# A two-layer graph network kernel: the second layer's PSUM banks and the steps of its dense sums

## The chip, the cores and the metric

The kernel runs on one core of one Trainium2 chip. The metric is the device time of one execution in microseconds (us); lower is better. Before the change three runs took 3727.17, 3734.83 and 3735.6 us, median 3734.83 us. A core has a matrix engine (PE; its weight loads are listed as PEld), a vector engine (DVE), a scalar engine (ACT), GpSimd (POOL) and SyncE (SP, which issues DMAs here). Each runs its own list of instructions strictly in order, and they meet through semaphores. PE writes its products to PSUM, which has eight banks of 128 x 512 fp32; DVE and ACT read them there.

## The reference, cut to what matters

```python
xn = layernorm(x)                                   # 6250 x 256
norm = w * rsqrt(deg_out[src] * deg_in[dst] + eps)  # 206250 edges
h6 = relu(segment_sum((xn @ W6)[src] * norm, dst) + b6)
h7 = relu(segment_sum((h6 @ W7)[src] * norm, dst) + b7)
x  = x + (h7 @ Wp + bp) + linear_attention(xn)
x  = x + mixture_of_experts(layernorm(x))           # 2 of 8 experts, 256 -> 512 -> 256
```

The change touches the second of the two `segment_sum` lines and what is computed beside it.

## The kernel before, in words

The edges are sorted by destination and cut into tiles of 128. A sum over edges is done in two ways at once.

*Run groups.* For 36 groups of 24 tiles in the second layer, POOL gathers the 128 source rows of each tile from DRAM by an indirect DMA (L1954, four per step, into a ring `msg` of six steps). PE multiplies the rows by small 128 x 32 matrices `Sb` (function `mm`, L659, four products a step) that DVE makes two steps ahead (`equal`, `weigh_S`, L1213 and L1228). After six steps a group is read by ACT, transposed by PE (`turn`, L647) and added by DVE to a sliding window `acc` (L1244).

*Dense chunks.* 26 chunks of edges are written as a whole matrix A (6250 sources by 128 destinations) and multiplied with the features X that lie in SBUF: 50 products per chunk, each 125x128 by 125x256 (function `dense`, L698; a product of fp32 operands is two instructions in the trace, so a chunk has 100). They add up in one PSUM bank, number 3. Then comes what I call the **boundary** of a chunk: ACT copies the bank to SBUF (`lift_chunk`, L1709), PE transposes it twice back into bank 3 (`dense_turn`, L706 and L708), DVE adds it to `acc` (`add_chunk`, L1253), and only then may the next chunk's first product write bank 3: `dense` waits for that addition.

21 of the 26 matrices were stored in DRAM in layer 1. SP loads each again (`load_A`, L2033, two DMAs of 1.6 MB) into one of two buffers, once the chunk before last is multiplied. Five ("extra groups" in the title) are built during layer 2: DVE makes one-hot matrices (`hots1`, L1274 and L1276), PE multiplies them (`build`, L676, 24 per chunk, four a step over six steps), and ACT evicts the results into A (`evict`, L1729 to L1735). Their builds take two banks in turn, 4 and 5.

*The stream.* As the windows of `acc` are complete, blocks of four row tiles (13 of them) go through the rest of the layer, one segment a step: `scl`, `hid0`, `relu0`, `hid1`, `relu1`, `out0`, `add0`, `out2`, `add2` with `stat`, `aggr`, `inv`, `norm`, `tr0`, `cp0`, `tr1`, `cp1`. PE's parts are L803 (hid, bank 2), L815 and L818 (out, bank 6) and L827 (tr, bank 7). The last block has banks 0, 1 and 3.

The order of work is fixed by hand in steps. Layer 2 has 234 steps, 0 to 233; steps 0 to 215 have an `mm`. Tables made at the top of the file tell which step does what: `AT1[c]` is the step at which chunk c starts (4, 12, 20, 28, ... up to 214), `MULT_AT[1]` holds the dense products of each step, `BUILD_AT[1]` the builds, `FIN_AT[1]` the boundary, `STREAM_AT` the stream. Every engine goes through the same steps. Before the change chunk c is multiplied in the steps `AT1[c] + 1` to `AT1[c + 1] - 1`, seven products in most steps; ACT lifts it at the end of that last step, and PE turns it and DVE adds it in step `AT1[c + 1]`, in which no dense product stands. Within a step PE does `mm`, one build, the turn of a chunk, two dense products, the turn of a run group, the other dense products and builds, and then the stream:

```python
if s < NQS[L]:
    mm(L, s)
for t in b[:1]:
    build(t)
if s in FIN_AT[L]:
    dense_turn(L, FIN_AT[L][s])
for d, k in m[:2]:
    dense(L, d, k)
```

Of the kernel before, what the change touches and what calls it, by code (L numbers as in the profile page):

```python
# [11 lines left out]
P = 128  # L12
W = 32
QT = 4
R = 125
# [100 lines left out]
FROM1 = 4  # L116
SPAN1 = NQS[1] - 2 - FROM1
assert NX == NY
# [25 lines left out]
for _c, _d in enumerate(CH[1]):  # L144
    if _d >= DY:
        for _t in range(size_of(_d)):
            BUILD_AT[1].setdefault(AT1[_c - 1] + 1 + _t * YB // size_of(_d), []).append(tile_of(_d) + _t)
    for _k in range(NT):
        MULT_AT[1].setdefault(AT1[_c] + 1 + _k * (AT1[_c + 1] - AT1[_c] - 1) // NT, []).append((_c, _k))
    FIN_AT[1][AT1[_c + 1]] = _c  # L150
PARTS = [("r", j) for j in range(NR)] + [("c", d) for d in range(DX)]
# [117 lines left out]
def gnn_block(nc, srcT, srcR, dstT, dstR, dstO, wO, wT, x, W6, b6, W7, b7, Wp, bp, wkvT, woT, wq, bo, lng, lnb,  # L269
              Wr, br, W1, b1, W2, b2, gamma, beta, need, out):  # L270
    ctx = ExitStack()
    with ctx:
# [251 lines left out]
        def bank_of(t):  # L524
            return (4, 5)[t % 2] if t >= tile_of(DY) else (2, 7, 5)[t % 3]

        def banks(t):
            return 2 if t >= tile_of(DY) else 3

# [41 lines left out]
        def pe_program(e):  # L571
# [107 lines left out]
            def dense(L, d, k):  # L679
                wd = XC if L == 0 else D  # L680
                if k == 0:
                    if L == 0:
                        e.wait_ge(s_ev, tile_of(d + 1))
                        e.wait_ge(s_r0, r0_before(tile_of(d + 1)))
                        e.wait_ge(s_xs, NT)
                    else:
                        e.wait_ge(l_xr, 16 * 5)
                    if L == 0 and d >= 1:
                        e.wait_ge(s_add, ADD_NO[0]["c", d - 1] + 1)
                    if L == 1 and d >= 1:  # L690
                        e.wait_ge(s_add, NU[0] + ADD_NO[1]["c", CH[1][d - 1]] + 1)
                    if L == 1 and CH[1][d] >= DY:
                        e.wait_ge(s_ev, tile_of(CH[1][d] + 1))
                        e.wait_ge(s_r0, r0_before(tile_of(CH[1][d] + 1)))
                if L == 1 and k % 25 == 0 and CH[1][d] < DY:
                    e.wait_ge(l_ap[(ND + d) % 2][k // 25], 16 * loaded(d))
                lhs = A[d % 2 if L == 0 else (ND + d) % 2][:, k, :]
                ins = e.matmul(PS[3][:, 0:wd], lhs, X[0:R, k, 0:wd], start=k == 0, stop=k == NT - 1)  # L698
                if k % 10 == 9:
                    ins.then_inc(s_mul, 1)  # L700

            def dense_turn(L, d):
                bank = PS[3]
                e.wait_ge(s_lc, L * ND + d + 1)
                if L == 0:
                    e.matmul(bank[:, 2 * P:3 * P], agd[:, D:D + 1].to_broadcast([P, P]), ident[:, :], start=True, stop=True)  # L706
                for h in range(2):
                    ins = e.transpose(bank[:, h * P:(h + 1) * P], agd[:, h * P:(h + 1) * P], ident[:, :])  # L708
                ins.then_inc(s_tc, 1)

            def sums(L, s):
# [4 lines left out]
                for t in b[:1]:  # L716
                    build(t)
                if s in FIN_AT[L]:
                    dense_turn(L, FIN_AT[L][s])
                for d, k in m[:2]:  # L720
# [69 lines left out]
            def stream(c, seg, slowly):  # L790
                (i0, n), k = CHUNKS[c], c % 2
                j, ci = half(c)
                wd, c0 = n * R, base_col(i0 * R)
                B_hid, B_out, B_tr = (PS[b] for b in ((0, 1, 3) if j else (2, 6, 7)))
                if seg in ("hid0", "hid1"):
                    m = int(seg[-1])
                    if not slowly:
                        e.wait_ge(c_scl, c + 1)
                    if 2 * ci + m >= 1:
                        e.wait_ge(c_relu[j], 2 * ci + m)  # L800
                    for h in range(2):
                        rhs = accs[:, h, i0 * R:i0 * R + wd] if slowly else acc[:, h, c0:c0 + wd]
                        ins = e.matmul(B_hid[:, 0:wd], w7[:, h, m * P:(m + 1) * P], rhs, start=h == 0, stop=h == 1)  # L803
                    ins.then_inc(c_hid[j], 1)
# [91 lines left out]
        def dve_program(e):  # L896
# [351 lines left out]
            def add_chunk(L, d):  # L1248
# [3 lines left out]
                o, n = (acc if L else acc3)[:, :, bass.ds(b, P)], 2 if L else 3  # L1252
                e.tensor_tensor(o, o, PS[3][:, 0:n * P].rearrange("p (h c) -> p h c", h=n), ALU.add).then_inc(s_add, 1)  # L1253
                added[0] += 1
# [358 lines left out]
        def act_program(e):  # L1613
# [90 lines left out]
            def lift_chunk(L, d):  # L1704
                wd = XC if L == 0 else D
                e.wait_ge(s_mul, 5 * (L * ND + d + 1))
                if L * ND + d >= 1:
                    e.wait_ge(s_tc, L * ND + d)
                e.activation(agd[:, 0:wd], PS[3][:, 0:wd], ACT.Copy).then_inc(s_lc, 1)  # L1709

# [90 lines left out]
            with e.Else():  # L1801
# [3 lines left out]
                for s in range(STEPS0):  # L1805
# [9 lines left out]
                    if s in HID_AT:  # L1815
                        degree_root(HID_AT[s])
                    if s + 1 in FIN_AT[0]:
                        lift_chunk(0, FIN_AT[0][s + 1])
                    for group in tables_at(0, s):
# [9 lines left out]
            def stream(c, seg):  # L1829
                (i0, n), k = CHUNKS[c], c % 2  # L1830
                j, ci = half(c)
                wd = n * R
                B_hid, B_tr = (PS[0], PS[3]) if j else (PS[2], PS[7])
                if seg in ("relu0", "relu1"):
# [22 lines left out]
            with e.Else():  # L1857
                for s in range(STEPS1):
# [4 lines left out]
                    for c, seg in STREAM_AT.get(s, ()):  # L1863
                        stream(c, seg)
                    if s + 1 in FIN_AT[1]:
                        lift_chunk(1, FIN_AT[1][s + 1])
                    clear1(s)
# [382 lines left out]
```

## Time and profile before

| | |
|---|---|
| median of three runs | 3734.83 us (3727.17 to 3735.6) |
| the profiled execution's own time | 3725.99 us |
| its span, first to last instruction | 3724.2 us |
| granted clock of PE over the span | 0.907 of full speed |
| PE busy with products | 2986.8 us (80%) |
| POOL busy | 2168.3 us (58%) |
| DVE busy, ACT busy | 1807.5 us (49%), 1147.4 us (31%) |

Times inside the trace are counted from the start of the span. The products of layer 2 begin at 2034.9 us, its last dense product ends at 3318.8 us, and from about 3350 us on the experts run. The clock is one of two levels, 1.0 (2.4 GHz) or 0.5 (1.2 GHz); a mean between them tells how long each was granted. The start of a product is recorded, its end is modelled, and the signal that tells the other engines of it can come later than that end.

### The profile page before, as it was taken

Reading aid. Unit: us, or ns where it says so; the run is one execution under the profiler, and the core shown is the slowest. Engines: PE = TensorE matmul, PEld = TensorE weight load, DVE = VectorE, ACT = ScalarE, POOL = GpSimd, SP = SyncE. Lnnn points to the kernel's source line nnn. Section 1 sums busy time; section 2 is a strip of 40 time slices with the busy share of each in tenths; the row PEclk is TensorE's granted clock in tenths of the full one; section 3 lists DMA queues with packets and bytes.
Section 4 is the critical chain, followed back from the end, with each engine's and each line's share of the span. In section 5 each row is a group of like instructions: output and inputs, shape, how many; then the busy total and the mean of one; then the engine's idle time right before and its main releaser. Section 6 shows DMA issues by size and latency. Waiting matters only on the chain.

```text
span 3724.2 us, 52328 instructions
## 1 busy us (share of the span) xinstructions
PE 2986.8 (80%) x16152; PEld 1996.9 (54%) x16152; DVE 1807.5 (49%) x4528; ACT 1147.4 (31%) x4063; POOL 2168.3 (58%) x2090
## 2 busy tenths in 40 slices
PE   4777837888888888878874688888888888888998
PEld 3445514555555555555542356555555555555666
DVE  9989835666666666656542133223222424222334
ACT  5777834443444444444330011001000101002211
POOL 4666656666666777666664666665666666630000
PEclk8899967998999999999996789889988989998999
DMA  4331134544545445445455535553555454533221
GB/s 118 98 102 57 56 78 132 173 140 137 173 138 163 150 139 173 135 142 167 129 194 177 124 126 168 192 187 106 193 193 191 148 192 149 190 101 106 78 77 47
DMA packets 219543, 515.58 MB, mean 138 GB/s; under 512 B 62465, under 2 KB 129831, under 8 KB 208169
## 3 DMA queue, kind: packets, MB, share of 16 engines
q0 software_dynamic: 88704, 243.35, 22.8%
q1 hardware_dynamic: 124053, 262.34, 20.7%
q10 hardware_dynamic: 6500, 6.40, 0.6%
q8 instruction: 141, 2.31, 0.2%
q14 instruction: 145, 1.19, 0.1%
HBM read 384.88 MB, written 127.07 MB: 137 GB/s over the span
## 4 chain that ended last, share of the span: by engine, by line
PE 33%; another core or an unknown queue 11%; issue 4%; DVE 3%; DMA 1%; ACT 1%; DVEq 0%; POOL 0%; SPq 0%; ACTq 0%; POOLq 0%
PE ps L698 13%; PE ps L867 5%; PE ps L880 4%; PE ps L659 3%; PE ps L676 3%; PE ps L818 1%; PE ps L815 1%; PE ps L803 1%; PE ps L708 0%; PE ps L638 0%; DVE wb L1274 0%; PE ps L827 0%; DVE accb L1244 0%; DVE ab L1297 0%
## 5 line engine op out<-in xcount | busy, mean ns | idle before, releaser
L1954 POOL DMA_INDIRECT ringb<-t,src x1848 | 1859.2, 1006 | 984.6 <-issue 494.6
L698 PE MATMUL ps<-xb,ab 125*128 125x256 f32 (+1 forms) x4700 | 1229.6, 402 | 87.3 <-issue 85.4
L698 PEld LDWEIGHTS ps<-xb,ab 125*128 125x128 f32 x4700 | 927.6, 201 | 355.1 <-issue 194.0
L676 PE MATMUL ps<-mlb 128*125 128x300 f32 x1260 | 476.9, 470 | 160.7 <-ACT side L1735 63.0
L1731 ACT ACTIVATE ab<-ps 125x250 f32 x724 | 294.7, 407 | 827.8 <-PE ps L676 410.7
L659 PE MATMUL ps<-ringb,Sb 128*32 128x257 f32 (+1 forms) x3696 | 358.7, 419 | 112.5 <-issue 46.3
L676 PEld LDWEIGHTS ps<-mlb 128*125 128x125 f32 x1260 | 224.6, 201 | 324.1 <-issue 281.6
L1927 POOL TENSOR_TENSOR ab<-ab,wn 128x100 f32<-128x100 f32 x201 | 274.1, 1369 | 169.5 <-DVE ab L1080 169.5
L600 PE MATMUL ps<-ab 128*50 128x125 f32 x3228 | 221.4, 284 | 135.6 <-ACT ab L1653 47.3
L1264 DVE TENSOR_TENSOR mlb<-iof,rel 128x900 f32<-128x900 f32 (+1 forms) x231 | 232.3, 1006 | 186.7 <-remote 129.9
L1653 ACT ACTIVATE ab<-ab,wn 128x50 f32<-128x50 f32 x1212 | 286.8, 328 | 21.1 <-DVE ab L1080 21.0
L600 PEld LDWEIGHTS ps<-ab 128*50 128x50 f32 x3228 | 180.6, 131 | 199.9 <-issue 100.5
L1213 DVE TENSOR_TENSOR Sb<-iof,rel 128x128 f32<-128x128 f32 x462 | 131.2, 284 | 292.4 <-remote 147.8
L1297 DVE TENSOR_TENSOR ab<-ab,side 125x50 f32 x724 | 177.6, 245 | 167.8 <-DVE ab L1297 77.0
L659 PEld LDWEIGHTS ps<-ringb,Sb 128*32 128x32 f32 x3696 | 86.2, 111 | 312.4 <-issue 235.8
L1082 DVE TENSOR_TENSOR ab<-iof,ringb 128x1000 f32<-128x1000 f32 x202 | 247.8, 1227 | 0.0
L1244 DVE TENSOR_TENSOR accb<-accb,ps 128x96 f32 (+1 forms) x308 | 73.8, 240 | 351.1 <-remote 248.3
L1959 POOL TENSOR_TENSOR rs<-mv,consts 125x4 f32<-125x4 f32 (+1 forms) x13 | 12.9, 989 | 394.4 <-DVE mv L1600 394.4
L1745 ACT ACTIVATE mlb<-mlb,wn 128x125 f32<-128x125 f32 x630 | 207.0, 393 | 92.7 <-issue 55.2
L867 PE MATMUL ps<-xb 128*128 128x500 f32 (+1 forms) x416 | 172.1, 572 | 4.1 <-DMA Sb<-in_b 3.6
L880 PE MATMUL ps<-xb,ab 128*125 128x256 f32 x800 | 174.6, 379 | 0.0
L880 PEld LDWEIGHTS ps<-xb,ab 128*125 128x125 f32 x800 | 150.2, 188 | 26.9 <-issue 5.1
(245 smaller groups left out, 2704.3 us busy)
## 6 DMA issues: line engine op xcount, KB each, us to landing
ad<-ab SPq DMA_DIRECT2D x42, 1600.0 KB
ab<-ad SPq DMA_DIRECT2D x42, 1600.0 KB
ringb<-t,src POOLq DMA_INDIRECT x1848
kvd<-mlb SPq DMA_DIRECT2D x50, 256.0 KB, 2.1
kvb<-kvd SPq DMA_DIRECT2D x50, 256.0 KB
x2t<-mlb SPq DMA_DIRECT2D x13, 500.0 KB
xb<-x2t SPq DMA_DIRECT2D x13, 500.0 KB, 8.2
xb<-in_x SPq DMA_DIRECT2D x10, 625.0 KB
```

What stands on the lines that cost most here:

```text
L600: ins = e.matmul(PS[j % 2][o:o + NT, 0:R], hot_w[:, r, j, :], hot_lo[:, r, j, :], start=t0 + j < 2, stop=t0 + j >= T - 2)
L659: ins = e.matmul(PS[g % 2][k * W:(k + 1) * W, 0:wd], Sb[:, qi % NS, k, :], msg[:, slot * QT + k, 0:wd], start=r == 0, stop=r == GR - 1)
L676: e.matmul(PS[bank_of(t)][0:R, 0:HR], low[:, slot_of(t), :], high[:, slot_of(t), :], start=True, stop=True).then_inc(s_bld, 1)
L698: ins = e.matmul(PS[3][:, 0:wd], lhs, X[0:R, k, 0:wd], start=k == 0, stop=k == NT - 1)
L867: ins = e.matmul(PS[j][:, 0:wd], M1[:, k, h, j * P:(j + 1) * P], XF[c % RF][:, h, 0:wd], start=h == 0, stop=h == 1)
L880: ins = e.matmul(pb[0:R, t * D:(t + 1) * D], hT[:, rr, m, (t0 + t) * R:(t0 + t + 1) * R], M2[:, m // 4, m % 4, :], start=m == 0, stop=m == 7)
L1082: e.tensor_tensor(hot_lo[:, r, 0:n, :], iof[:, 0:R].unsqueeze(1).to_broadcast([P, n, R]), lo_f[:, t0:t0 + n].unsqueeze(2).to_broadcast([P, ...
L1264: e.tensor_tensor(Mb[:, o:o + n, :], iof[:, 0:HR].unsqueeze(1).to_broadcast([P, n, HR]), rel[:, c0:c0 + n].unsqueeze(2).to_broadcast([P, n ...
L1653: e.activation(hot_w[:, r, j, :], hot_hi[:, r, j, :], ACT.Copy, scale=wn[:, t0 + j:t0 + j + 1]).then_inc(s_wa, 1)
L1731: e.activation(A1[place][:, :, bass.ds(b, RT - 1)], bank[:, :, 1:RT], ACT.Copy).then_inc(s_ev, 1)
L1927: e.tensor_tensor(hot_w[:, c % RD, NA:n, :], hot_hi[:, c % RD, NA:n, :], wn[:, t0 + NA:t0 + n].unsqueeze(2).to_broadcast([P, n - NA, NT]), ...
L1954: e.indirect_dma_start(msg[:, slot * QT + k, 0:width], None, table, bass.IndirectOffsetOnAxis(src[:, t:t + 1], 0)).then_inc(s_g[slot], 16)
```

## The change

It applies to the second layer alone (L = 1); for layer 1 every table and bank stays.

- *Dense chunks* alternate between banks 3 and 7. Chunk c waits for the addition of chunk c - 2 instead of c - 1. The products now fill the steps `AT1[c]` to `AT1[c + 1] - 1`, so none is left out, with six or seven a step. `FIN_AT` moves two steps on: ACT lifts chunk c in step `AT1[c + 1]`, PE turns it in `AT1[c + 1] + 1` (`FIN_AHEAD`), DVE adds it in `AT1[c + 1] + 2`. `AT1` is spread over one step less (the last chunk ends in step 212 instead of 213).
- *The stream* of all blocks but the last uses bank 6 for hid, out and tr. `hid0` of a block waits in addition until ACT has copied `cp1` of the block before.
- *Builds* of the five extra groups take banks 2, 4 and 5 in turn; a build waits for the eviction of the third before it instead of the second.

```diff
-SPAN1 = NQS[1] - 2 - FROM1
+SPAN1 = NQS[1] - 3 - FROM1
...
-        MULT_AT[1].setdefault(AT1[_c] + 1 + _k * (AT1[_c + 1] - AT1[_c] - 1) // NT, []).append((_c, _k))
-    FIN_AT[1][AT1[_c + 1]] = _c
+        MULT_AT[1].setdefault(AT1[_c] + _k * (AT1[_c + 1] - AT1[_c]) // NT, []).append((_c, _k))
+    FIN_AT[1][AT1[_c + 1] + 2] = _c
+FIN_AHEAD = [0, 1]
...
         def bank_of(t):
-            return (4, 5)[t % 2] if t >= tile_of(DY) else (2, 7, 5)[t % 3]
+            return (2, 4, 5)[t % 3] if t >= tile_of(DY) else (2, 7, 5)[t % 3]
+
+        def dense_bank(L, d):
+            return (3, 7)[d % 2] if L else 3
 
         def banks(t):
-            return 2 if t >= tile_of(DY) else 3
+            return 3
...
-                    if L == 1 and d >= 1:
-                        e.wait_ge(s_add, NU[0] + ADD_NO[1]["c", CH[1][d - 1]] + 1)
+                    if L == 1 and d >= 2:
+                        e.wait_ge(s_add, NU[0] + ADD_NO[1]["c", CH[1][d - 2]] + 1)
...
-                ins = e.matmul(PS[3][:, 0:wd], lhs, X[0:R, k, 0:wd], start=k == 0, stop=k == NT - 1)
+                ins = e.matmul(PS[dense_bank(L, d)][:, 0:wd], lhs, X[0:R, k, 0:wd], start=k == 0, stop=k == NT - 1)
...
-                if s in FIN_AT[L]:
-                    dense_turn(L, FIN_AT[L][s])
+                if s + FIN_AHEAD[L] in FIN_AT[L]:
+                    dense_turn(L, FIN_AT[L][s + FIN_AHEAD[L]])
...
-                B_hid, B_out, B_tr = (PS[b] for b in ((0, 1, 3) if j else (2, 6, 7)))
+                B_hid, B_out, B_tr = (PS[b] for b in ((0, 1, 3) if j else (6, 6, 6)))
...
                         e.wait_ge(c_relu[j], 2 * ci + m)
+                    if m == 0 and ci >= 1:
+                        e.wait_ge(c_cp[j], 2 * ci)
...
-                    if s + 1 in FIN_AT[1]:
-                        lift_chunk(1, FIN_AT[1][s + 1])
+                    if s + 1 + FIN_AHEAD[1] in FIN_AT[1]:
+                        lift_chunk(1, FIN_AT[1][s + 1 + FIN_AHEAD[1]])
```

`dense_turn`, `add_chunk`, `lift_chunk` and ACT's half of the stream take the same new banks.

## Rows read from the trace of the kernel before

**Rows 1.** The profile's page: span and busy times.
```profile
span 3724.2 us, 52328 instructions
PE 2986.8 (80%) x16152; PEld 1996.9 (54%) x16152; DVE 1807.5 (49%) x4528; ACT 1147.4 (31%) x4063; POOL 2168.3 (58%) x2090
...
q8 instruction: 141, 2.31, 0.2%
```

**Rows 2.** Busy time by stretch: length, each engine (instructions), clock, DMA share, GB/s.
```profile
2034.90:2126.00 91.10, 51.34 (x221) 28.97 (x222) 10.13 (x35) 3.95 (x4) 60.84 (x64) 0.67 0.57 139
2126.00:3319.00 1193.00, 1001.49 (x4984) 688.22 (x4983) 343.56 (x1118) 119.44 (x372) 765.31 (x793) 0.91 0.51 165
```

**Rows 3.** PE's waits, 2100 to 3330: total us, times, longest.
```profile
PE ps L698 <- issue: 68.8, 68, 5.0
PE ps L708 <- ACT agd L1709: 46.9, 11, 9.7
PE ps L659 <- issue: 24.8, 37, 2.2
PE ps L676 <- DVE wb L1276: 14.4, 8, 5.5
PE ps L676 <- DVE wb L1274: 10.4, 7, 5.0
PE ps L676 <- ACT side L1735: 8.4, 5, 5.2
PE ps L708 <- issue: 6.6, 4, 3.0
```

**Rows 4.** POOL's gathers by source line, 2100 to 3330: durations, then idle before.
```profile
L1954 POOL DMA_INDIRECT ringb<-t,src x809: 943/949/1922, 2099.7 to 3309.3; - x162
...
  issue: 218.0, 711
  remote: 123.4, 53
  PE ps L659: 87.9, 45
```

**Rows 5.** Busy time in the ten boundaries shorter than 5 us.
```profile
2405.35:2409.27 3.92, 1.51 (x19) 0.48 (x19) 0.52 (x3) 0.66 (x2) 3.00 (x4) 1.00 0.89 287
...
sum 34.76, PE 22.71 PEld 7.83 DVE 7.94 ACT 7.46 POOL 23.55; mean PE 2.27 PEld 0.78 DVE 0.79 ACT 0.75 POOL 2.36
```

**Rows 6.** Busy time in the fifteen boundaries of 5 us and more.
```profile
2212.76:2225.01 12.25, 3.40 (x22) 1.41 (x22) 3.64 (x13) 3.14 (x2) 7.64 (x8) 0.60 0.30 86
...
2497.88:2506.42 8.54, 1.61 (x20) 0.48 (x19) 1.26 (x8) 0.68 (x2) 6.41 (x8) 0.74 0.75 263
...
sum 136.33, PE 58.18 PEld 25.52 DVE 25.23 ACT 24.48 POOL 86.90; mean PE 3.88 PEld 1.70 DVE 1.68 ACT 1.63 POOL 5.79
```

**Rows 7.** Timeline of one boundary: start, length, engine, line, idle before.
```profile
2495.56 2.33 PE L698 MATMUL ps<-xb,ab 125*128 125x256 f32 x10
...
2500.68 0.80 SPq L2033 DMA_DIRECT2D ab<-ad  x2
2500.68 0.38 ACT L1709 ACTIVATE agd<-ps 128x256 f32<-128x256 f32 x1 [2.31 <-remote]
...
2501.12 0.44 PE L708 MATMUL ps<-ident,agd 128*128 128x128 f32 x2 [2.66 <-ACT agd L1709]
...
2505.89 0.42 DVE L1253 TENSOR_TENSOR accb<-accb,ps 128x256 f32 x1 [7.17 <-remote]
...
2506.42 6.55 PE L698 MATMUL ps<-xb,ab 125*128 125x256 f32 x16 [4.26 <-issue]
...
2513.47 3.30 PE L698 MATMUL ps<-xb,ab 125*128 125x256 f32 x14
```

**Rows 8.** Timeline: a block's cp1 on ACT, the next block's hid0 on PE.
```profile
2530.86 0.20 ACT L1848 ACTIVATION_READ_ACCUMULATOR mlb<-ps 128x1 f32 x1
...
2543.64 1.90 PE L803 MATMUL ps<-accb,kvb 128*128 128x500 f32 x4
```

More of the change, by code:

```diff
@@ L702, in dense_turn @@
             def dense_turn(L, d):
-                bank = PS[3]
+                bank = PS[dense_bank(L, d)]
                 e.wait_ge(s_lc, L * ND + d + 1)
@@ L1252, in add_chunk @@
                 o, n = (acc if L else acc3)[:, :, bass.ds(b, P)], 2 if L else 3
-                e.tensor_tensor(o, o, PS[3][:, 0:n * P].rearrange("p (h c) -> p h c", h=n), ALU.add).then_inc(s_add, 1)
+                e.tensor_tensor(o, o, PS[dense_bank(L, d)][:, 0:n * P].rearrange("p (h c) -> p h c", h=n), ALU.add).then_inc(s_add, 1)
                 added[0] += 1
@@ L1708, in lift_chunk @@
                     e.wait_ge(s_tc, L * ND + d)
-                e.activation(agd[:, 0:wd], PS[3][:, 0:wd], ACT.Copy).then_inc(s_lc, 1)
+                e.activation(agd[:, 0:wd], PS[dense_bank(L, d)][:, 0:wd], ACT.Copy).then_inc(s_lc, 1)
             tile_columns = TileColumns(e, "at")
@@ L1816, in act_program @@
                         degree_root(HID_AT[s])
-                    if s + 1 in FIN_AT[0]:
-                        lift_chunk(0, FIN_AT[0][s + 1])
+                    if s + 1 + FIN_AHEAD[0] in FIN_AT[0]:
+                        lift_chunk(0, FIN_AT[0][s + 1 + FIN_AHEAD[0]])
                     for group in tables_at(0, s):
@@ L1832, in stream @@
                 wd = n * R
-                B_hid, B_tr = (PS[0], PS[3]) if j else (PS[2], PS[7])
+                B_hid, B_tr = (PS[0], PS[3]) if j else (PS[6], PS[6])
                 if seg in ("relu0", "relu1"):
```

## The prediction

> **What bounds the kernel now.** I read the page first, then busy time by stretch, then the waits of PE and of POOL in layer 2, then the boundaries between dense chunks one by one. The page shows PE as the busiest engine, 2986.8 us of a span of 3724.2 us, POOL next with 2168.3 us [rows 1]. The change touches only layer 2. Its dense part runs from 2034.9 to about 3319 us, 1284.1 us in two stretches: 91.1 us of start, in which PE is busy for 51.34 us at a mean clock of 0.67, and 1193 us in which it is busy for 1001.49 us at 0.91 [rows 2].
>
> Who holds whom in those 1193 us? A step has four gathers of 949 ns, and at least 0.30 us lies before each (218.0 us over 711 waits), so POOL needs 4 x 1.25 = 5.0 us a step; 216 steps are 1080 us, against the 1284 us that they take. The rest is POOL waiting: 123.4 us for a releaser that the trace can't name and 87.9 us for PE's products L659, 211 us in all, which are waits for a free place in the ring [rows 4]. Among PE's waits of the same stretch none is for a gather; they are for its own issue, for ACT's lift L1709, and for the builds' inputs [rows 3]. So PE sets the pace, and POOL is up to a ring behind it with some 200 us to spare. What PE saves in this stretch comes off the end, until POOL's 1080 us are reached.
>
> PE loses time at the boundaries. From the end of a chunk's last dense product to the start of the next chunk's first there are 25 of them: ten short ones of 34.76 us with 22.71 us of PE work (run-group products, turns, stream) [rows 5], fifteen long ones of 136.33 us with 58.18 us [rows 6]. Idle: 12.05 and 78.15 us, 90.2 us together. The timeline of one shows the chain: the last products end at 2497.89, ACT lifts at 2500.68, when the signal has come (SP starts the next load of A at the very same time, so it is the signal that is late and not ACT), PE turns at 2501.12, DVE adds at 2505.89 to 2506.31, and the next dense product starts at 2506.42, at the lower clock: 16 instructions in 6.55 us, where 14 take 3.30 us at full clock later, which is 3.77 us for 16 [rows 7].
>
> **The change part by part.**
>
> *Dense banks in turn, boundary two steps later.* Removed are the wait for the addition of the chunk just done and, as far as one step of PE work covers it, the wait of the turn for the lift. No instruction is added to PE: 50 products, two transposes, one lift and one addition a chunk, as before. What goes has three terms.
> 1. What every boundary costs, even where the signal is prompt: 12.05 / 10 = 1.2 us idle [rows 5]. 25 x 1.2 = 30 us. The lift (0.38 us), the turn and the addition (0.42 us) now lie beside dense products of the other bank. I take all of it.
> 2. What the late signals add at the long ones: 78.15 - 15 x 1.2 = 60 us [rows 6]. Here I have to choose. If the lateness belongs to the round trip from PE to ACT to PE to DVE to PE, all 60 us go. If PE itself is held up (it waits 68.8 us in dense products and 24.8 us in run products on nothing but issue [rows 3]), the delay comes back inside a chunk, where the gain is 0. I can't tell them apart, and take half, 30 us.
> 3. The clock. Behind the boundary of [rows 7] the 16 instructions cost 6.55 - 3.77 = 2.8 us more. Twelve of the fifteen long boundaries have a mean clock under 0.90 (between 0.60 and 0.89; two of them stand in [rows 6]), so up to 12 x 2.8 = 34 us. It goes with the idle time of term 2; half, 17 us.
> Sum: 77 us. From both sides: term 1 alone, 30 us, if the delays return; 30 + 60 + 34 = 124 us if everything goes.
>
> *Next behind the turn.* The turn stands after `mm` and one build of the step after the lift, and a step of six or seven dense products and an `mm` is some 4 us of PE work at full clock (14 instructions in 3.30 us and the `mm`). The longest wait of the turn for the lift is 9.7 us [rows 3], so a rest of up to some 5 us stays at the worst boundaries; that is inside the half of term 2.
>
> *Loads of A.* The load of chunk c still starts when chunk c - 2 is multiplied, but chunk c starts one step earlier, eight steps later instead of nine. Two DMAs of 1.6 MB at the 287 GB/s of the boundary stretch at 2405 us [rows 5] are about 11 us against eight steps of at least 5.0 us. Cost 0; if the cover were gone, PE would wait for the second half of A. SP's queue issues it at the same place, and no other DMA moves by more than a step.
>
> *Stream in one bank.* Inside a block the bank was already handed on by waits (relu before the next hid, add before the next out, norm before tr), so the one new wait is `hid0` for the `cp1` before. In the trace cp1 of a block ends at 2531.06 and the next block's first hid product starts at 2543.64 [rows 8]: 12.6 us of slack over two steps. Behind this wait on PE stand the run products, for which POOL waits. I price it at 0; were all the slack gone, each of the 11 such waits would cost at most the part of a step that ACT is late. The banks 2 and 7 that it frees are what makes the other two edits possible.
>
> *Builds in three banks.* PE waits 14.4 + 10.4 us before builds for DVE's one-hot matrices, which three banks don't change, and 8.4 us for ACT's eviction (L1735), which they may take away [rows 3]. Against it stands that PE no longer gives DVE a pause before the builds of the five extra chunks: five boundaries' 1.2 us, 6 us, may come back as waits for DVE. I take -2 us for the two together, between a gain of 8 and a loss of 6.
>
> *Start and end.* Dense products begin in step 4 instead of 5, in a stretch where PE is busy for 56% [rows 2]: a gain of a few us at most, 0 in the sum, since the 91 us there are set by gathers and a low clock. The last chunk ends a step earlier and is added a step later (215 for 214), before the stream's step 216 that needs it: 0. The number of steps stays 234.
>
> Sum: 77 - 2 = 75 us. 3725.99 - 75 = 3651 us for an execution like the profiled one; the median of the runs before, 3734.83, lies 8.8 us above that execution, so the forecast is 3734.8 - 75 = **3660 us**.
>
> *A rule against it.* POOL's spare time says that PE's idle time at boundaries is on the path [rows 4]. The Trainium skill, "TensorE: Matmul & The Clock Gate", section "HAM oscillation — how this bites in real kernels", reports of a tuned matmul kernel that double-buffering its PSUM gave no further gain (125.5 after 126.6 us); by that the sum would be about 0. That is rival 3. On term 2, the skill's "Runtime: NRT & Kernel Launch", section "Instruction fetch mechanics", holds that the cost of crossing a 16 KiB block of instructions is mostly hidden; 2.31 MB in 141 packets on the instruction queue q8 [rows 1] are such blocks. By that PE's waits on issue would not be its own supply, and all of term 2 would go (rival 1).
>
> **The rivals.**
> 1. *All of it goes*: 124 us and the 8 us of evictions, 3735 - 130 = 3605 us. For it: ACT and SP see the signal late together, and a pause in PE's work stands before each low clock. Against: issue waits also stand in the middle of chunks [rows 3].
> 2. *Only the fixed part goes*, 30 us, less the 6 us at extra chunks: 3711 us. For it: 93.6 us of issue waits that no bank explains [rows 3].
> 3. *No gain*: what PE saves it waits for elsewhere, for gathers or DVE, 3735 us. For it: the ring couples PE and POOL, and the load of A now meets a running PE with DMA shares of 0.75 to 0.92 [rows 5, 6]. Against: 1080 us of gathers against 1284 us.
> 4. *Slower*: the lift now follows ACT's stream segment of the step `AT1[c + 1]`. In 11 of the 26 boundaries that is a relu or a copy (steps 36, 52, 68, 84, 100, 116, 132, 180, 188, 204, 213), which itself waits for PE. If each held the turn, and with it the run products behind it, by as much as the longest wait of today, 9.7 us [rows 3], that is 107 us against the 75 gained: 3767 us. It decides once such a wait is over 6.8 us each. Against: each of these segments waits for a PE segment one step earlier.
>
> **How the numbers follow.** Forecast (gain of 45 to 110 us) 0.60; rival 1 0.10; rival 2 0.14; rival 3 0.09; rival 4 0.07. About 0.3%, 11 us, is what a measurement of this kernel can tell from no change. Rival 2 is mostly faster by that bound: faster 0.60 + 0.10 + 0.12 = 0.82, within 0.3% 0.02 + 0.08 = 0.10, slower 0.01 + 0.07 = 0.08. The range goes from 3608, nearly all of rival 1, to 3720, rival 2 with a margin of 9 us; outside remain rivals 3 and 4 and a tail of rival 1, some 0.2. The forecast's own range is 3625 to 3690.
>
> **What would show it.** In the trace after: PE's wait before L708, 53.5 us now (46.9 + 6.6), under 15 us, and no idle time of PE tied to L1253; the boundary stretches close to pure PE work; the stretch from the first run product to the last dense product down from 1284 to about 1210 us with a mean clock above 0.91; POOL's 211 us of waits down by about as much; builds' waits near 33 us; the time from the last dense product to the end unchanged. It is wrong if L708 waits as long as now (rival 4), if issue waits of L698 and L659 grow by what L708 loses (rival 2), or if PE begins to wait for gathers (rival 3).

## The result, and the profile after

The kernel after takes 3711.0 us (five runs, 3708.81 to 3720.0), the kernel before 3734.83 (five runs, 3727.17 to 3737.23): ratio 0.9946, 95% interval 0.9935 to 0.9958. It is 24 us faster, clear of the noise; the forecast was 75. The profiled execution of after is the slowest of its five (3720.0 us), that of before (3725.99) lies under all of its five, so the two traces lie only 6 us apart, and differences of a few us are not read from them.

The page of after, first lines [rows 1]:

```profile
span 3718.2 us, 52328 instructions
PE 3030.2 (81%) x16152; PEld 2012.8 (54%) x16152; DVE 1803.2 (48%) x4528; ACT 1150.8 (31%) x4063; POOL 2172.4 (58%) x2090
```

The same instructions, yet PE is "busy" for 43 us more. Layer 2's two stretches, columns as in [rows 2]:

```profile
2036.80:2128.00 91.20, 52.46 (x233) 30.55 (x234) 9.01 (x32) 3.53 (x3) 61.02 (x64) 0.67 0.59 140
2128.00:3311.00 1183.00, 1028.47 (x4953) 690.00 (x4952) 339.33 (x1116) 119.00 (x370) 767.85 (x792) 0.90 0.52 166
```

The second is 10 us shorter. PE's idle time in it fell from 191.5 to 154.5 us, its busy time rose from 1001.5 to 1028.5, and the clock did not rise (0.91, 0.90). PE's waits, 2100 to 3330 us: total, times, longest [rows 3]:

```profile
PE ps L702 <- issue: 59.0, 75, 1.8
PE ps L663 <- issue: 58.9, 75, 2.4
PE ps L680 <- DVE wb L1280: 9.6, 4, 5.5
...
PE ps L680 <- DVE wb L1282: 4.1, 3, 1.6
...
PE ps L712 <- ACT agd L1715: 1.9, 2, 1.5
PE ps L712 <- issue: 1.3, 3, 0.6
```

L702 is before's L698 (dense), L663 its L659 (run products), L680 its L676 (builds), L712 its L708 (turn). The wait of the turn is gone, 53.5 us to 3.2. What came in its place stands in the second line: run products wait 58.9 us on their issue ("issue": PE waits for nothing that the trace shows), 24.8 before. And POOL waits as much as ever for its ring, 137.5 + 64.3 = 201.8 us against 211.3 [rows 4] ("remote": a signal whose sender the trace can't name):

```profile
POOL ringb L1960 <- issue: 219.4, 715, 1.0
POOL ringb L1960 <- remote: 137.5, 60, 3.7
POOL ringb L1960 <- PE ps L663: 64.3, 36, 4.9
```

The timeline of after around the lift of one chunk (start, length, engine, line, idle before) answers to [rows 7]:

```profile
2507.30 0.38 PE L663 MATMUL ps<-ringb,Sb 128*32 128x256 f32 x1 [1.06 <-issue]
...
2509.40 0.38 PE L663 MATMUL ps<-ringb,Sb 128*32 128x256 f32 x1 [1.73 <-issue]
...
2510.11 1.11 PE L663 MATMUL ps<-ringb,Sb 128*32 128x256 f32 x4 [0.33 <-issue]
2510.21 0.79 SPq L2039 DMA_DIRECT2D ab<-ad  x2
2510.22 0.39 ACT L1715 ACTIVATE agd<-ps 128x256 f32<-128x256 f32 x1 [2.94 <-remote]
2510.31 0.29 DVE L1219 TENSOR_TENSOR Sb<-iof,rel 128x128 f32<-128x128 f32 x1 [0.98 <-remote]
2510.55 0.95 POOL L1960 DMA_INDIRECT ringb<-t,src  x1 [2.61 <-remote]
...
2511.14 0.69 PE L712 MATMUL ps<-ident,agd 128*128 128x128 f32 x2
```

The eight run products of one step, which have nothing to wait for between them, take from 2505.55 to 2511.22, in pieces. The last dense product of the chunk that is lifted ends at 2501.20, yet the trace has its signal at 2510.19, and ACT's lift, which waits for it, starts at 2510.22, 9.0 us late. SP, ACT, DVE and POOL all move within 0.34 us of each other. So two things are late: PE's own starts, and its signals to everyone, the latter also for products behind which PE went on for 4 us without a hole. Such holes also stand between dense products of one chunk: successive starts are 0.216 us apart at full clock and 0.427 at half, but 49 times over 0.6 us in before and 70 times in after, which by the starts in the traces costs 45 and 68 us beyond the usual distance.

The same lateness is what POOL waits for. In before the median distance from one gather's start to the next is 1.25 us; the 1284.5 us from the first of the 864 gathers to the last contain 87 pauses of over 2.2 us at the first gather of a step, the one that waits for PE's run products, and these hold 182 us more than 1.25 us each. Counted by the recorded ends of the products, the place in the ring had been free for 5.7 us (median) when such a pause ended; 81 of the 87 end 0.2 to 0.4 us after a recorded signal of PE's run products. In after it is 84 pauses with 175 us.

### The profile page after: what moved, and what is told of

It is laid out like the page before. It is cut to its first block, busy times and chain, and to the rows that moved or that the text cites. A ratio compares the mean times of both kernels' runs of the same rounds, so it can differ in the third digit from the quotient of the medians.

```text
span 3718.2 us, 52328 instructions
## 1 busy us (share of the span) xinstructions
PE 3030.2 (81%) x16152; PEld 2012.8 (54%) x16152; DVE 1803.2 (48%) x4528; ACT 1150.8 (31%) x4063; POOL 2172.4 (58%) x2090
## 4 chain that ended last, share of the span: by engine, by line
PE 46%; issue 8%; another core or an unknown queue 6%; DVE 3%; DMA 2%; ACT 1%; POOL 1%; DVEq 1%; ACTq 0%; SPq 0%; POOLq 0%
PE ps L702 19%; PE ps L680 7%; PE ps L663 5%; PE ps L873 5%; PE ps L886 4%; PE ps L821 1%; PE ps L824 1%; POOL ringb L1960 1%; PE ps L642 1%; PE ps L809 1%; ACT ab L1737 1%; DMA t<-mbuf 0%; DVE ab L1303 0%; DMA x2d<-accb 0%
## 5 line engine op out<-in xcount | busy, mean ns | idle before, releaser
L702 PE MATMUL ps<-xb,ab 125*128 125x256 f32 (+1 forms) x4700 | 1253.7, 407 | 83.3 <-issue 80.6
L702 PEld LDWEIGHTS ps<-xb,ab 125*128 125x128 f32 x4700 | 934.9, 203 | 358.5 <-issue 197.7
L680 PE MATMUL ps<-mlb 128*125 128x300 f32 x1260 | 484.1, 475 | 170.4 <-issue 67.9
L663 PE MATMUL ps<-ringb,Sb 128*32 128x257 f32 (+1 forms) x3696 | 378.2, 417 | 141.9 <-issue 78.2
L680 PEld LDWEIGHTS ps<-mlb 128*125 128x125 f32 x1260 | 228.1, 205 | 335.7 <-issue 298.1
L663 PEld LDWEIGHTS ps<-ringb,Sb 128*32 128x32 f32 x3696 | 90.5, 111 | 362.3 <-issue 290.3
```

The costliest lines, as they stand in the source:

```text
L663: ins = e.matmul(PS[g % 2][k * W:(k + 1) * W, 0:wd], Sb[:, qi % NS, k, :], msg[:, slot * QT + k, 0:wd], start=r == 0, stop=r == GR - 1)
L680: e.matmul(PS[bank_of(t)][0:R, 0:HR], low[:, slot_of(t), :], high[:, slot_of(t), :], start=True, stop=True).then_inc(s_bld, 1)
L702: ins = e.matmul(PS[dense_bank(L, d)][:, 0:wd], lhs, X[0:R, k, 0:wd], start=k == 0, stop=k == NT - 1)
```

## The experiments

Two kinds of chips took part, and the kernel before ran on each beside the experiments. On two "prompt" chips it took 3372.5 and 3370.9 us, on three "late" chips 3726.1, 3736.3 and 3734.5, as in the result. The names say only how soon PE's signals arrive in the traces. Ratios are to the kernel before on the same chip.

| run | chip | us | ratio, 95% interval |
|---|---|---|---|
| dense_alone | prompt 1 | 3371.5 | 0.9996 (0.9987 to 1.0004) |
| rest_alone | prompt 1 | 3373.2 | 1.0000 (0.9991 to 1.0008) |
| b_1g / a_1g | prompt 1 | 3225.9 / 3220.6 | 0.9565 (0.9551 to 0.9579) / 0.9543 (0.9527 to 0.9559) |
| change | prompt 2 | 3363.0 | 0.9976 (0.9965 to 0.9986) |
| b_lag | prompt 2 | 3368.4 | 0.9993 (0.9983 to 1.0003) |
| b_1g_lag / a_1g_lag | prompt 2 | 3297.6 / 3216.3 | 0.9780 (0.9765 to 0.9794) / 0.9539 (0.9525 to 0.9554) |
| b_ahead3 | late 1 | 3724.6 | 0.9992 (0.9980 to 1.0004) |
| a_ahead3 | late 1 | 3705.5 | 0.9950 (0.9926 to 0.9975) |
| b_1g_lag18 / a_1g_lag18 | late 1 | 3619.7 / 3520.1 | 0.9720 (0.9701 to 0.9739) / 0.9449 (0.9428 to 0.9470) |
| b_nold | late 2 | 3736.3 | 0.9997 (0.9986 to 1.0008) |
| a_nold | late 2 | 3720.0 | 0.9958 (0.9942 to 0.9975) |
| b_2g / a_2g | late 2 | 3400.7 / 3388.2 | 0.9098 (0.9078 to 0.9118) / 0.9061 (0.9046 to 0.9076) |
| b_5dense | late 3 | 3708.1 | 0.9917 (0.9886 to 0.9948) |
| b_3g | late 3 | 3487.1 | 0.9338 (0.9320 to 0.9356) |

**The halves of the change.** dense_alone is the kernel after with builds in two banks and the stream in 2, 6, 6; rest_alone is the kernel before with only the new banks of stream and builds.

```diff
 # dense_alone, from after
-            return (2, 4, 5)[t % 3] if t >= tile_of(DY) else (2, 7, 5)[t % 3]
+            return (4, 5)[t % 2] if t >= tile_of(DY) else (2, 7, 5)[t % 3]
...
-            return 3
+            return 2 if t >= tile_of(DY) else 3
...
-                B_hid, B_out, B_tr = (PS[b] for b in ((0, 1, 3) if j else (6, 6, 6)))
+                B_hid, B_out, B_tr = (PS[b] for b in ((0, 1, 3) if j else (2, 6, 6)))
...
```

> The dense chunks' part alone: banks 3 and 7 in turn, products in all steps, boundary two steps later. The stream keeps bank 2 for hid and has bank 6 for out and tr; builds keep two banks. Theory A (most of what the boundaries lost comes back as PE's own issue waits, and the bank sharing costs nothing): the whole gain of the change, 20 to 26 us, so 3709 to 3715 us. Rival B (the dense part brings 75 us and sharing bank 6 or the builds take 50 back): 3655 to 3675 us.

> The other two parts alone: the stream's products share bank 6 with the added wait, builds take banks 2, 4, 5; the dense chunks as before. Theory A: no change beyond 5 us, 3730 to 3740 us. Rival B: slower by some 50 us, 3785 us.

Neither moves the time on this chip. The expectations were written for a kernel before of 3735 us, so this does not decide between A and B; the halves ran on no late chip, and which of them brings the 24 us there is not shown. Waits of rest_alone in layer 2 (1900 to 2990 us), PE's and then POOL's:

```profile
PE ps L659 <- DMA ringb<-t,src: 100.7, 48, 7.0
PE ps L676 <- DVE wb L1276: 5.1, 6, 1.1
PE ps L698 <- issue: 1.7, 7, 0.5
```

```profile
POOL ringb L1956 <- issue: 249.7, 819, 0.3
POOL ringb L1956 <- PE ps L659: 4.6, 15, 0.3
```

Here PE waits for gathers, POOL for nothing but its own issue, and there are no holes. The gathers set the pace: their median distance is 1.25 us, as in before, but only 2 pauses are longer than 2.2 us. What PE saves at a boundary, it waits for at the next gather.

**PE in front.** b_1g and a_1g issue one gather of four in layer 2, so that PE is the last on any chip.

```diff
-                    for k in range(QT):
+                    for k in range(1 if L else QT):
...
```

PE's wait for the gathers is set to the smaller number in the same way.

> The kernel before with one of the four gathers of each step in layer 2, as in a_1g. The difference to a_1g is what the change is worth when PE alone sets the pace. Theory C: 50 to 100 us slower than a_1g (each of the 25 boundaries costs its 1.2 us idle, a part of the late signals and of the clock). If the difference is 20 to 30 us as on the full kernels, the boundaries never cost more than that, and the gathers took nothing back.

> The changed kernel with one of the four gathers of each step in layer 2; the other three are left out, so three quarters of the run groups' rows are stale. Theory C (PE's issue waits come while POOL issues gathers without a pause, and end when POOL has to wait): with a quarter of the gathers POOL waits in every step, the issue waits of PE in layer 2 (118 us) shrink to under 30 us, the clock stays high, and layer 2 runs near PE's work, some 945 us at full clock from the first run product to the last dense one: 3400 to 3470 us. Rival D (the issue waits are PE's own supply of instructions): the same number of instructions, so the issue waits stay at some 100 us, and the time is over 3600 us.

The difference of the two kernels is 5.3 us, where b_1g's expectation had 50 to 100. The 3400 to 3470 us of a_1g's theory C were meant for a late chip, and this chip has no holes to take away, so that run does not decide between C and D. Busy time by stretch of b_1g: one boundary, and the sum over its 25:

```profile
1959.68:1961.38 1.70, 1.51 (x19) 0.47 (x19) 0.42 (x1) 0.66 (x2) 0.83 (x1) 1.00 0.63 120
sum 71.77, PE 65.75 PEld 28.44 DVE 27.76 ACT 31.03 POOL 25.34; mean PE 2.63 PEld 1.14 DVE 1.11 ACT 1.24 POOL 1.01
```

71.77 - 65.75 = 6.0 us of idle time, 0.24 us a boundary, at full clock: that is all that a boundary costs where signals are prompt, and the change returns it.

**An artificial late signal.** Six more lifts ahead of the one that counts:

```diff
+                for r in range(6 if L else 0):
+                    e.activation(agd[:, 0:wd], PS[3][:, 0:wd], ACT.Copy).then_inc(s_lag, 1)
+                    e.wait_ge(s_lag, 6 * d + r + 1)
                 e.activation(agd[:, 0:wd], PS[3][:, 0:wd], ACT.Copy).then_inc(s_lc, 1)
```

> The kernel before with one gather of four a step in layer 2 (three quarters of its products read stale rows), and six more lifts of each of layer 2's chunks ahead of the one that counts, each waiting for the one before: an artificial late signal of about 6 x 0.5 = 3 us in each of the 25 boundaries, in a kernel in which PE sets the pace. Theory B (the boundary of the kernel before puts the whole of PE's idle time at each boundary on the path, and it is 0.24 us in each where signals are prompt): 25 x 3 = 75 us more than the 3225.9 us without the lag, 3290 to 3310 us. Rival R (a lag is made up by work queued elsewhere, so a late signal costs little even in the kernel before): under 3245 us.

> The same six more lifts for each chunk, and one gather of four, in the kernel after. Theory B: the turn stands a step, 4.3 us of PE work, behind the lift, so a lag of 3 us is covered nearly everywhere: within 8 us of the 3220.6 us without it. Rival S (the lag is not covered, because ACT starts the lift late in its step behind its stream segment or behind evictions): 30 us or more.

> The kernel before with all four gathers and the same six more lifts a chunk. Theory G at a kernel before of about 3370 us: in the dense part of 1061 us PE is busy for 962, so POOL's pace hides part of the 75 us: 5 to 45 us more. Where the kernel before takes about 3730 us and PE sets the pace: 60 us or more. Rival P (PE sets the pace on this chip too): 75 us more whatever the chip.

b_1g_lag pays 71.7 us, 2.9 a boundary; a_1g_lag nothing (-4.3; the two runs without the lag were on the other prompt chip). Theory B holds: where PE sets the pace, a late lift is paid in full before and hidden after. PE's wait for the lift in b_1g_lag, then in a_1g_lag:

```profile
PE ps L709 <- ACT agd L1713: 53.2, 26, 2.5
```

```profile
PE ps L713 <- ACT agd L1719: 2.0, 1, 2.0
```

b_lag has the same 25 late lifts, and PE waits 47.8 us for them in the dense part, but with all four gathers the time doesn't move at all. I had expected 5 to 45 us. The wait for gathers shrinks instead, from 100.7 us in rest_alone to 51.4:

```profile
PE ps L660 <- DMA ringb<-t,src: 51.4, 29, 4.5
PE ps L709 <- ACT agd L1713: 47.8, 25, 2.5
```

How far does the cover reach? Eighteen more lifts:

> The kernel before with one gather of four a step in layer 2 and eighteen more lifts of each chunk ahead of the one that counts. Six of them cost 71.7 us (3297.6 against 3225.9), 2.9 us in each of 25 boundaries; eighteen make a signal that is 8.6 us late, near the longest wait for a lift in the kernel before (9.7 us). Theory B: 3226 + 25 x 8.6 = 3441 us, 3425 to 3455. Rival R: under 3400 us.

> The same eighteen more lifts in the kernel after, one gather of four. Theory B with the price that the prediction put on a long signal (the turn stands a step of 4.3 us and a run product behind the lift, some 5 us in all): 8.6 - 5 = 3.6 us stay at each of 25, so 3216 + 90 = 3306 us, 3285 to 3330. Rival T (the cover is longer, up to two steps, because the work between is at least two steps): under 3235 us. Rival S (no cover left once the signal is later than the step): over 3400 us.

These ran on a late chip, where layer 1 with all its gathers takes 160 us more, so the totals miss what I wrote and the dense part is compared (b_1g_lag18, then a_1g_lag18):

```profile
2048.40:3208.00 1159.60, 978.37 (x5148) 691.91 (x5148) 345.26 (x1140) 294.96 (x824) 199.25 (x204) 0.91 0.32 105
```

```profile
2051.10:3110.00 1058.90, 966.00 (x5145) 689.31 (x5146) 343.77 (x1138) 294.71 (x823) 201.69 (x205) 0.95 0.35 115
```

Without lag the two take 930 and 924 us. So a signal that costs 230 / 25 = 9.2 us before costs 135 / 25 = 5.4 after: the change covers 3.8 us of lateness at each boundary. The prediction had some 5 us of cover. Theory B had 215 and 90 us for the two; it is right in kind, but the 135 us of after lie over its range of 69 to 114. R, S and T fall. With one gather of four neither trace has a hole between dense products, though the chip is a late one.

**The whole change on a prompt chip.**

> The change as a whole, run again beside the kernel before, since the times of the experiments' first chip (3372.5 us for the kernel before) differ by a tenth from those in which the change brought 24 us (3734.8 us). Theory G (POOL's gathers set the pace of layer 2 where no signal is late: 1061 us of dense part against 216 steps at about 5.2 us of gathers): a ratio of 0.998 to 1.001 if the kernel before takes about 3370 us again. If the kernel before takes about 3730 us: 0.993 to 0.996. Rival W (the whole is worth more than its two halves, which measured 0.9996 and 1.0000): a gain of 10 us or more at 3370 us.

8 us faster, 5 to 12 by its interval. Theory G had a ratio of 0.998 or more, Rival W a gain of 10 us or more; it lies between, and the interval reaches both. From first to last dense product it takes 1057 us, against 1062 and 1063 for the halves on the other prompt chip. The trace nearest to the kernel before on this chip is that of b_lag, at 0.9993 of its time: in both, layer 2's run products begin at 1865 us, and the last dense product ends at 2949.6 in change and at 2958.3 in b_lag, so the gain lies inside the dense part. Why the whole brings what neither half does is not shown.

**A shorter lead of POOL.**

```diff
-                        e.wait_ge(s_mm, L * NQ + j - RQ + 1)
+                        e.wait_ge(s_mm, L * NQ + j - (3 if L else RQ) + 1)
...
```

> The kernel before with POOL's gathers of layer 2 kept at most three steps ahead of PE's run products instead of six (the ring's depth). It asks what the ring's spare places hide. Theory G (POOL sets the pace and PE follows it closely, so the ring is seldom more than three steps full): within 10 us of the kernel before. Rival H (what a late PE costs is made up out of the ring's six places; with three, each of the 25 boundaries reaches POOL): 15 to 50 us slower. Where the kernel before takes about 3730 us, theory C (PE is held up while POOL runs on through a dozen gathers, and a shorter lead breaks this up): 20 us faster or more; its rival there: slower.

> The kernel after with the same lead of three steps. Theory G: within 10 us of the kernel before, and within 8 us of b_ahead3. Rival H: faster than b_ahead3 by 15 us or more, since the boundary that reaches POOL there is gone here.

Nothing moves: b_ahead3 as before, a_ahead3 0.9950 as the change itself, 19 us under b_ahead3. Theory C falls. Rival H falls for b_ahead3, which should have been 15 to 50 us slower; that a_ahead3 is 15 us or more faster, as it had it, is only the gain that the change has without the shorter lead. Theory G holds for b_ahead3 and misses a_ahead3 (within 8 us). The holes are fewer (30 of over 0.6 us instead of 49, and 20 in a_ahead3), and PE waits 72.9 us for gathers instead, 104.4 in a_ahead3. POOL pauses as before, 90 times for 184 us. That was the first sign that on a late chip, too, something other than PE's work keeps the time.

**The loads of A, and half of the gathers.** b_nold and a_nold leave out layer 2's refills of A; b_2g and a_2g issue two gathers of four.

```diff
...
-                if s in refill:
-                    load_A(refill[s])
```

> The kernel before without layer 2's refills of A (19 chunks are multiplied with what the two buffers held): all four gathers. If the kernel before takes about 3726 us: theory Y: the holes go, and the dense part falls to POOL's pace of about 1100 us, 3560 to 3620 us in all; theory X: it stays within 40 us of the kernel before. If the kernel before takes about 3372 us: POOL's pace is unchanged, 3350 to 3375 us.

> The kernel after without layer 2's refills of A. Theory X at 3726 us: 15 to 30 us under b_nold, as the full kernels are. Theory Y at 3726 us: within 10 us of b_nold, as both then follow POOL. At a kernel before of 3372 us: within 8 us of b_nold.

> The kernel before with two gathers of four a step in layer 2 (half of its products read stale rows). POOL then needs 216 x 2.5 = 540 us and PE sets the pace. If the kernel before takes about 3726 us: theory X (holes come with the gathers' rate): the dense part falls from 1257 to 930 to 1000 us, 3400 to 3470 us in all, with few holes; theory Y (the loads of A bring them): the dense part stays over 1100 us, 3570 or more. If the kernel before takes about 3372 us there are no holes to explain, and PE's pace gives 3226 us, as with one gather, 3220 to 3240.

> The kernel after with two gathers of four. Under theory X, or at a kernel before of 3372 us, its advantage over b_2g is that of prompt boundaries, 0.24 x 25 = 6 us, 2 to 12 us. Under theory Y at 3726 us it is that of the full kernels, 15 to 30 us.

Theory Y falls, and the loads have no part in it: b_nold has the time of before, its holes (39) and its waits, and a_nold is 16 us under it. Half of the gathers gone, every hole is gone. Dense part of b_2g, then POOL's waits and PE's:

```profile
2059.00:2990.00 931.00, 920.55 (x5148) 660.45 (x5148) 345.03 (x1140) 123.21 (x374) 400.34 (x408) 1.00 0.49 159
```

```profile
POOL ringb L1954 <- PE ps L659: 408.5, 167, 7.2
...
POOL ringb L1954 <- issue: 84.2, 223, 4.4
```

```profile
PE ps L698 <- issue: 3.0, 14, 0.5
```

This is how a stretch looks in which PE does set the pace: 99% busy, clock 1.00, nearly all of POOL's waiting named after PE's product, no "remote". POOL issues its next gather a median of 0.3 us after the product that frees the place; in the kernel before it is 5.3 us after it. Theory X, that the holes come with the rate of the gathers, holds; it says nothing of how. The change is worth 12.5 us in total here, just over the 2 to 12 expected, and 6.8 us in the dense part (931.0 to 924.2). The two profiled executions lie only 2.7 us apart, so they can't tell where the other 6 are.

**Which way the link runs.** b_5dense keeps every gather and load and takes 45 of 50 dense products of each chunk away.

```diff
+                if L == 1 and k % 10 != 9:
+                    return
...
```

b_3g issues three gathers of four.

> The kernel before with 5 of 50 dense products in each chunk of layer 2 (the dense sums lack the other 45), all four gathers, all loads. PE's work in the dense part falls by about 1170 x 2 x 0.216 = 505 us, so PE can't set the pace. If the kernel before takes about 3735 us: theory Z (the gathers have a pace of 1.49 us each of their own): the time stays within 25 us of the kernel before, 3705 to 3745. Theory V (PE's dense work and the gathers disturb each other): the gathers go at the 1103 us of the other chips, 3540 to 3570 us. If the kernel before takes about 3372 us: within 10 us of it, as POOL's gathers set the pace.

> The kernel before with three gathers of four. If the kernel before takes about 3735 us: theory Z: 648 x 1.49 = 964 us from the first gather to the last, near PE's own 930 us of dense part, so 3400 to 3440 us and few holes. Theory V with a disturbance that grows with the gathers: the dense part half way between 930 and 1257 us, 3500 to 3600 us. If the kernel before takes about 3372 us: 648 x 1.28 = 827 us, below PE's 930, so PE's 3226 us, 3220 to 3240.

With nearly all dense work gone the time falls by 26 us, to 3708 us. PE's dense part, PE's waits and POOL's:

```profile
2075.60:3304.00 1228.40, 637.30 (x2804) 289.22 (x2800) 348.28 (x1141) 123.28 (x375) 805.08 (x832) 0.66 0.53 166
```

```profile
PE ps L659 <- issue: 118.6, 97, 5.8
PE ps L659 <- DMA ringb<-t,src: 68.4, 20, 18.1
PE ps L710 <- ACT agd L1711: 63.5, 8, 16.5
```

```profile
POOL ringb L1956 <- issue: 230.3, 755, 0.5
POOL ringb L1956 <- remote: 132.6, 42, 5.8
POOL ringb L1956 <- PE ps L659: 46.6, 20, 8.5
```

PE is idle for half of it, and still every engine waits for late signals, PE's turn for ACT's lift for 16.5 us at worst. One such place in the timeline of b_5dense:

```profile
2209.06 0.59 PE L659 MATMUL ps<-ringb,Sb 128*32 128x256 f32 x1 [0.83 <-issue]
...
2216.55 0.94 POOL L1956 DMA_INDIRECT ringb<-t,src  x1 [0.30 <-issue]
2221.94 0.38 ACT L1711 ACTIVATE agd<-ps 128x256 f32<-128x256 f32 x1 [28.08 <-remote]
2221.96 0.94 POOL L1956 DMA_INDIRECT ringb<-t,src  x1 [4.46 <-remote]
2222.10 1.28 DVE L1246 TENSOR_TENSOR accb<-accb,ps 128x64 f32 x4 [13.12 <-remote]
2222.38 0.69 PE L710 MATMUL ps<-ident,agd 128*128 128x128 f32 x2 [12.74 <-issue]
```

The last dense product of the chunk that ACT lifts ends at 2202.02, the run products that free the place for which POOL waits (those of step 26) at 2197.94, and PE's last product before the gap at 2209.64. ACT, POOL, DVE and PE go on together at 2221.94 to 2222.38; the trace has the signal of that dense product at 2221.92, 19.9 us late.

The gathers take as long as before. Their line by source, with first and last start at its end, in before, b_5dense and rest_alone (prompt):

```profile
L1954 POOL DMA_INDIRECT ringb<-t,src x864: 943/949/1922, 2024.8 to 3309.3; - x173
```

```profile
L1956 POOL DMA_INDIRECT ringb<-t,src x864: 940/946/1957, 2035.0 to 3299.3; - x173
```

```profile
L1956 POOL DMA_INDIRECT ringb<-t,src x864: 942/949/1992, 1862.4 to 2963.1; - x173
```

1284.5, 1264.3 and 1100.7 us. On late chips it is between 1264 and 1289 us in all seven kernels with four gathers (after 1279.2, b_ahead3 1284.9, a_ahead3 1276.8, b_nold 1288.6, a_nold 1279.7), whatever PE has to do. Theory Z has the time right (3708 in 3705 to 3745), theory V falls. But what Z says of the reason, a pace of 1.49 us that the gathers have of their own, the traces refute: in each of these kernels the median distance between gathers is 1.25 us, as on the prompt chips, and the rest is pauses at the ring, 182 us in before and 166 us in b_5dense (55 pauses, and there the place had been free for 15.5 us). The same holds for b_3g, which by Z should have had 964 us of gathers and 3400 to 3440 us, and by V 3500 to 3600; it has

```profile
L1954 POOL DMA_INDIRECT ringb<-t,src x648: 943/949/1969, 2028.5 to 3066.9; - x162
```

1038 us and 3487 in all, with some holes back (PE waits 16.1 us on the issue of dense products). Its median distance is 1.25 us, too, with 96 pauses at the ring; in about half of them POOL goes on within 0.6 us of the product that frees the place, so there PE's work does set the pace, and in the others the signal is late.

## Why the prediction was wrong

- *"So PE sets the pace ... What PE saves in this stretch comes off the end, until POOL's 1080 us are reached"* is the step that failed. I took POOL's 211 us of waits for the ring as slack behind PE's work. They were waits for late signals of products that had ended 5.7 us (median) earlier, so a PE that is done sooner ends them little sooner: with 90% of the dense work gone (b_5dense) the gathers still take 1264 us, not 1080, and the whole kernel loses 26 us (19 to 43 by its interval). The change brought 24. b_5dense keeps the kernel before's boundaries, so its 3708 us are what less PE work brings, and no floor for other arrangements of the waits; the change together with 5 dense products of 50 was not run.
- *Term 1, 30 us for 1.2 us at each boundary*: mis-sized. Prompt boundaries cost 0.24 us each, 6 us in all (b_1g, and 6.8 us between b_2g and a_2g). That the other 0.96 us of each short one were late signals too is what this suggests; no run shows it by itself.
- *Term 2, half of 60 us of late signals*: the mechanism was right, since a late lift is paid in full before (71.7 us in b_1g_lag) and covered up to 3.8 us after, and the turn's wait is gone in the trace. But most of the time came back, for the reason of the first point: 34 us as issue waits of run products, and 27 us hidden inside PE's busy time. In two of three pairs on late chips that goes with more holes between dense products (49 to 70; 39 to 72 for b_nold and a_nold); in the third they got fewer (30 to 20 for b_ahead3 and a_ahead3), PE's busy time stayed, and PE waits longer for gathers instead (72.9 to 104.4 us). a_2g does the same work as b_2g in 1.4 us less of busy time, so the 27 us are not work. What is left over is alike in the three pairs: from the first run product to the last dense product 10, 14 and 14 us less (before to after, b_ahead3 to a_ahead3, b_nold to a_nold).
- *Term 3, 17 us of clock*: nothing came. The mean clock went from 0.91 to 0.90. It is 1.00 in b_2g, which has no such pauses; here they only moved.
- *Builds, -2 us*: waits before builds went from 33.2 to about 22 us (9.6 + 8.0 + 4.1 and under 1 for ACT), too little to tell from the rest. *Loads of A at 0*: right, neither run without them is faster than its partner with them. *Stream at 0*: rest_alone is 1.0000, but only on a prompt chip, where the gathers would hide a small cost; on a late chip it is open.
- The range given, 3608 to 3720, holds the 3711, but by rival 2's part of it; the forecast's own, 3625 to 3690, does not. *Rival 2* (3711 us) has the time by luck, and in part the sign it was to be known by: the issue waits of L698 and L659 together grow by 24.3 us, where L708 loses 50.3. It does not have the reason: no 30 us of fixed part exist. *Rival 3*'s reason, another pace than PE's, is the nearest, and I had set it aside with "1080 us of gathers against 1284 us". *Rival 4* did not occur: the turn's longest wait is 1.5 us.
- On the two rules that the prediction names. The Trainium skill, "TensorE: Matmul & The Clock Gate", section "HAM oscillation — how this bites in real kernels", has no further gain from double-buffering PSUM in its kernel. dense_alone, the dense chunks' part of the change with its second bank, agrees (0.9996), and here the trace shows the reason, a pace set by gathers; where PE sets the pace the whole change brings 5.3 and 12.5 us (a_1g, a_2g). The Trainium skill, "Runtime: NRT & Kernel Launch", section "Instruction fetch mechanics", has the cost of crossing an instruction block mostly hidden. The traces agree as far as they go: during layer 2's gathers the instruction queue q8 carries 43 packets in before and in rest_alone and 42 in b_2g, with holes or without, and in b_5dense only 25, with signals as late as ever; and the holes do not stand at these packets, in before 6 of the 49 overlap one in time, in after none of the 70. Yet term 2 did not go.

What stays open: what holds PE for 0.7 to 3 us between products, and its signals for longer, on some chips while gathers run at three or four a step, and not on others. The recorded landings of the gathers are not later for it (median 1.8 us after the end of the fourth gather in before, 2.8 in the prompt rest_alone). No kernel here is faster than the one after with all its work: a_ahead3's 0.9950 stands beside the change's own 0.9946.

## What to carry to other kernels

An engine sets the pace of another that waits for it only if the other goes on as soon as it is done. Before a saving is taken off the end, find the instruction that ends the other's wait, and look how long after it the other goes on: 0.3 us where the pace is there (b_2g), 5.3 us here. Price a boundary at its idle time in the best case, not at the mean of the short ones. And when several engines are idle together, one experiment that takes the suspected engine's work nearly away shows whether that work sets the time.

## What was not expected of the hardware

- The same kernel takes 3371 to 3373 us on two chips and 3726 to 3736 on three. Some 165 us of this lie ahead of layer 2 (its gathers start at 1862 and at 2025 us). In layer 2 the rest goes when gathers are left out: 930 us of dense part with one of four on a prompt chip (b_1g), 931 us with two of four on a late one (b_2g).
- It is not that a gather is slower: 1.25 us from one to the next (median) on both kinds. On the late chips some 170 to 190 us of pauses at the ring come to it, which end with late signals of PE.
- On the late chips PE stands still between products that wait for nothing, in pieces of about 0.7 us and its multiples, and the signals of its finished products reach ACT, SP, DVE and POOL together, in the rows above 9.0 us (after) and 19.9 us (b_5dense) late.
- The recorded busy time of PE contains such pauses: the same products were busy for 1001.5 and 1028.5 us.
